# Window attention scores on 32-row tiles of TensorE over four PSUM banks, with a three-bank ring for the other products

## Chip, core and metric

The kernel runs on one core of a Trainium2 chip. The metric is the device time of one execution in microseconds. The engines are TensorE (PE in the rows; its weight loads are PEld), VectorE (DVE), ScalarE (ACT), GpSimd (POOL) and SyncE (SP). Each works through its own list of instructions in order, and they wait for each other through semaphores. TensorE writes its results into PSUM, eight banks of 128 partitions by 512 float32.

## What is computed

Four blocks run one after the other on x of 16 samples, 96 channels and 16 by 16 pixels, each as x = x + block(group_norm(x)): layer 0 is window attention with 12 heads of width 8, layer 1 shifted-window attention with 12 heads of width 32, then two blocks of convolution (layer 2) and spiking attention (layer 3), whose arithmetic the change leaves alone. A sample has four windows of 64 tokens.

```python
# layer 0, hd = 8
attn = jnp.einsum('bhnd,bhmd->bhnm', q * scale, k)
attn = jax.nn.softmax(attn + bias[None], axis=-1)
out = jnp.einsum('bhnm,bhmd->bhnd', attn, v)
out = out @ proj_w.T + proj_b
# layer 1, HD = 32, on x rolled by (-4, -4); masks in two of the windows' halves
dots = jnp.einsum('bhwid,bhwjd->bhwij', q, k) * SCALE
dots = dots + pos_emb[REL[..., 0], REL[..., 1]]
attn = jax.nn.softmax(dots, axis=-1)
out = jnp.einsum('bhwij,bhwjd->bhwid', attn, v)
out = out @ w_out + b_out
```

## The kernel before

Everything stays in SBUF after the loads at the start; eight stores end the run. All attention arithmetic is float32. The two attention layers form one chain of 32 steps, one per sample, that every engine walks through with its own function (`pe_sample`, `act_sample`, `dve_sample`, `pool_sample`; `attention_layers` calls them, and a loop of two samples each covers the regular middle of a layer). A step handles sample s and, to keep all engines busy, parts of its neighbours: prev = s-1, prev2 = s-2, nxt = s+1, nxt2 = s+2.

The four windows of a sample are two pairs, and each pair gives two groups of six heads: four groups w = 0 to 3, in halves j = 0 (w = 0, 1) and j = 1 (w = 2, 3). A group passes through these operations:

- scores (`pe_scores`, L900): 12 matmuls for each half, each on 64 rows by 64 columns of the array with 128 moving columns. The 64 rows hold more than one head, so k is copied from PSUM once per head with a mask that zeroes the others (`evac_k`, L1050), and in layer 0 q is copied three times with three masks (`evac_q`, L1038).
- bias add (`dve_bias`, L1099), row maximum (`dve_max`, L1103), subtraction of the maximum on GpSimd (`pool_shift`, L1141),
- transposition, three 128 by 128 blocks (`pe_transpose`, L909), exponential (`act_exp`, L1005),
- values (`pe_values`, L929: 12 matmuls of 128 by 64), division by the row sums (`dve_heads`: reciprocal L1126, multiply L1128), turning the result (`pe_turn`, L958), the output product (`pe_out`, L975 and L973), its bias (`act_out`), and the residual on GpSimd.

The products q, k and v of a coming sample (`pe_qkv`, L866 for q and k, L876 for v) are spread between these. PSUM: banks 0 and 1 hold scores, 2 and 3 the transposed probabilities (`ps_probsT`, used in turn), 4 the values (`ps_heads`), 5 and 6 the q, k and v products in turn (`ps_qkv`, `bank_of`), 7 everything else (`ps_mix`: turned heads, output product, statistics, weight preparation). One semaphore per `ps_qkv` bank (`evac_a`, `evac_b`) counts the copies out of it.

A float32 matmul stands as two MATMUL and two LDWEIGHTS records in the trace, a transposition as one of each. So a scores step has 24 records of either kind.

TensorE's order in a step: scores j=1; values j=1 of prev; v of nxt; (layer 1: turn j=0 of prev;) transpose 0; (layer 1: third qk product of nxt;) transpose 1; output product of prev2; scores j=0 of nxt; values j=0; (layer 1: second v product;) transpose 2; first product of nxt2; transpose 3; turn of prev; second product of nxt2. VectorE's order is bias 2 and 3, maximum 2, then in layer 0 the division of prev, maximum 3 and the two v copies of nxt (L1062), in layer 1 the v copies, maximum 3 and the division; then the same kind of work for the j=0 scores of nxt.

Some steps carry a job as well: the group-norm statistics of a half layer (0,1), (1,0), (1,1), (2,0), or a piece of weight preparation ("pos", "pw", "w3", "bn", "pwT"). Each has a part on VectorE before the bias adds of nxt (`dve_job_in`), a TensorE part in `ps_mix`, and a part on VectorE at the step's end.

## Time and profile before

| | us |
|---|---|
| median of 3 runs | 401.65 (399.36 to 402.13) |
| the profiled execution | 399.56 |
| its span | 397.8 |
| layer 0 steps, from the first j=1 scores of sample 0 | 24.1 to 140.4 |
| layer 1 steps, to the j=1 scores of the last sample | 140.4 to 306.9 |
| the rest of the span (layers 2 and 3, stores) | 306.9 to 397.8 |

TensorE is busy for 92% of the span, VectorE for 77%, ScalarE for 61%, GpSimd for 46%. A busy share adds up records, and TensorE's matmuls overlap, so its share alone doesn't say that it bounds the kernel. The timeline, which lists groups of equal instructions by start time with the idle time before them, shows whether one follows the other without a gap. Times in it are from the start of the span.

### The profile page before, as it was taken

What the parts mean: (1) busy time and instruction counts of PE and PEld (TensorE: products, weight loads), DVE (VectorE), ACT (ScalarE), POOL (GpSimd) and SP (SyncE); (2) the same over time, 40 slices, a digit from 0 to 9 for tenths busy, and PEclk for the clock granted to TensorE, in tenths of its full rate; (3) what the DMA queues carried; (4) which work ended last, traced back from release to release, by engine and by line L of the source; (5) the groups of instructions that cost most, each with busy time, mean ns of one, the idle gap of its engine ahead of it and who ended that gap; (6) DMA issues with size and microseconds to landing.
All of it is one profiled execution on the core that took longest, in us unless ns stands there. A gap on an engine that the chain in (4) does not pass through costs nothing.

```text
span 397.8 us, 13249 instructions
## 1 busy us (share of the span) xinstructions
PE 365.8 (92%) x4889; PEld 266.8 (67%) x4889; DVE 306.5 (77%) x721; ACT 243.7 (61%) x571; POOL 184.0 (46%) x325
## 2 busy tenths in 40 slices
PE   4579999999999997999999999999999999998893
PEld 1458878888878775877787777787777643334441
DVE  4887877878788679788977777787887949878774
ACT  5346666666756566456555666655556635559992
POOL 6765775756677444254443443443544334341000
PEclk9999999999999999899999999999999999999998
DMA  7700000000000000000000000000000000000112
GB/s 159 139 5 4 4 2 2 0 0 0 2 2 2 2 3 1 2 4 1 4 2 0 0 0 0 0 0 0 4 0 4 0 2 0 0 0 3 50 50 59
DMA packets 8505, 5.09 MB, mean 13 GB/s; under 512 B 5034, under 2 KB 8234, under 8 KB 8466
## 3 DMA queue, kind: packets, MB, share of 16 engines
q1 hardware_dynamic: 8306, 4.56, 5.2%
q8 instruction: 26, 0.43, 0.4%
q14 instruction: 13, 0.11, 0.1%
q10 hardware_dynamic: 160, 0.00, 0.0%
HBM read 2.98 MB, written 1.57 MB: 11 GB/s over the span
## 4 chain that ended last, share of the span: by engine, by line
PE 74%; DVE 11%; issue 4%; ACT 4%; POOL 0%; POOLq 0%; ACTq 0%; DVEq 0%
PE bank L929 12%; PE bank L900 12%; PE bank L866 11%; PE bank L909 10%; PE bank L1423 7%; PE bank L876 7%; PE bank L973 5%; PE bank L958 4%; DVE row_max L1103 2%; PE bank L1428 2%; DVE v L1062 2%; PE bank L1523 1%; PE bank L975 1%; ACT kvT L1556 1%; ACT count L1532 1%
## 5 line engine op out<-in xcount | busy, mean ns | idle before, releaser
L1141 POOL TENSOR_TENSOR probs<-probs,row_max 128x384 f32<-128x384 f32 x128 | 105.4, 829 | 115.0 <-DVE row_max L1103 114.2
L1005 ACT ACTIVATE probsT<-bank 128x384 f32<-128x384 f32 x128 | 61.1, 492 | 74.4 <-PE bank L909 74.4
L1099 DVE TENSOR_TENSOR probs<-bank,bias 128x384 f32<-128x384 f32 x128 | 65.4, 552 | 51.3 <-PE bank L900 49.9
L1103 DVE TENSOR_REDUCE row_max<-probs 128x6 f32<-128x384 f32 x128 | 68.4, 545 | 1.0
L909 PE MATMUL bank<-cst,probs 128*128 128x128 f32 x384 | 63.0, 281 | 0.0
L929 PE MATMUL bank<-v,probsT 128*64 128x18 f32 (+1 forms) x1536 | 58.1, 220 | 3.2 <-DVE headsN L1128 2.9
L929 PEld LDWEIGHTS bank<-v,probsT 128*64 128x64 f32 x1536 | 50.5, 138 | 14.7 <-issue 13.6
L900 PE MATMUL bank<-k,q 64*64 64x128 f32 x1536 | 56.7, 277 | 1.9 <-ACT k L1050 1.9
L900 PEld LDWEIGHTS bank<-k,q 64*64 64x64 f32 x1536 | 41.3, 132 | 22.0 <-issue 21.0
L1050 ACT ACTIVATE k<-bank,cst 128x256 f32<-128x256 f32 x128 | 54.0, 483 | 1.7 <-PE bank L866 1.7
L909 PEld LDWEIGHTS bank<-cst,probs 128*128 128x128 f32 x384 | 44.7, 142 | 11.2 <-issue 4.7
L1062 DVE COPY v<-bank 64x384 f32<-64x384 f32 (+1 forms) x96 | 46.8, 487 | 4.1 <-PE bank L876 1.8
L866 PE MATMUL bank<-xn,w 128*128 128x256 f32 x192 | 49.7, 381 | 0.0
L866 PEld LDWEIGHTS bank<-xn,w 128*128 128x128 f32 x192 | 32.8, 191 | 2.5
L1151 POOL TENSOR_TENSOR x<-y_attn,x_turned 96x96 f32<-96x96 f32 (+3 forms) x64 | 18.4, 317 | 25.8 <-ACT y_attn L1021 25.8
L1423 PE MATMUL bank<-pad,tapT 96*96 96x512 f32 x64 | 28.9, 594 | 0.0
L1010 ACT COPY heads<-bank 128x384 f32<-128x384 f32 x32 | 15.5, 484 | 21.4 <-PE bank L958 21.3
L876 PE MATMUL bank<-w,xn 128*64 128x192 f32 x256 | 27.2, 333 | 0.0
L1032 ACT ACTIVATE q<-bank 128x256 f32<-128x256 f32 x48 | 18.8, 391 | 12.4 <-PE bank L866 12.4
L866 PE MATMUL bank<-xn,w0T 128*128 128x256 f32 x64 | 20.4, 405 | 6.5 <-ACT xn L998 4.2
L958 PE MATMUL bank<-cst,headsN 128*128 128x128 f32 (+1 forms) x128 | 23.0, 282 | 3.6 <-DVE gn_veps L755 2.7
L1128 DVE TENSOR_TENSOR headsN<-bank,inv_sum 128x384 f32<-128x384 f32 (+1 forms) x48 | 23.6, 491 | 1.7
(147 smaller groups left out, 514.8 us busy)
## 6 DMA issues: line engine op xcount, KB each, us to landing
x<-in_x SPq DMA_DIRECT2D x4, 384.0 KB, 5.6
out_dram<-x SPq DMA_DIRECT2D x8, 192.0 KB, 2.1
w<-in_L_conv_w_qkv SPq DMA_DIRECT2D x1, 432.0 KB, 5.3
cst<-in_consts SPq DMA_DIRECT2D x1, 304.0 KB, 5.3
p<-in_L_conv_w_out SPq DMA_DIRECT2D x1, 144.0 KB, 5.1
pos<-in_L_conv_pos_emb SPq DMA_DIRECT2D x8, 2.0 KB
cst<-in_consts SPq DMA_DIRECT2D x1, 117.0 KB, 2.2
w_raw<-in_L_conv_qkv_w SPq DMA_DIRECT2D x1, 108.0 KB, 5.0
```

Of the source, the lines that this page charges most:

```text
L866: last = nc.tensor.matmul(o[:, half * T:(half + 1) * T], w[:, col:col + 128], xn[par][:, :], start=True, stop=True)
L876: last = nc.tensor.matmul(o[h * WT:(h + 1) * WT, at_ * n:(at_ + 1) * n], xn[par][:, w * WT:(w + 1) * WT], w_v[:, h], start=True, stop=True)
L900: one = nc.tensor.matmul(ps_scores[u][c * WT:(c + 1) * WT, p * 128:(p + 1) * 128], q, k, start=True, stop=True)
L909: last = nc.tensor.transpose(ps_probsT[w % 2][:, p * 128:(p + 1) * 128], probs[w][:, 2 * p:2 * p + 2, :], ident)
L929: last = nc.tensor.matmul(ps_heads[c * WT:(c + 1) * WT, at_:at_ + n], probsT[2 * j + u][:, p * 128 + c * WT:p * 128 + (c + 1) * WT], v, st ...
L1005: nc.scalar.activation(probsT[w][:, :], ps_probsT[w % 2][:, 0:NP * 128], ACT.Exp).then_inc(L.s.probsT_sb, 1)
L1050: return nc.scalar.activation(dst, src, ACT.Copy, scale=scale)
L1062: return nc.scalar.copy(dst, src) if eng == "act" else nc.vector.tensor_copy(dst, src)
L1099: nc.vector.tensor_tensor(out, scores, b, ALU.add).then_inc(L.s.biased, 1)
L1103: nc.vector.tensor_reduce(row_max[w][:, :], probs[w][:, :, :], AX.X, ALU.max).then_inc(L.s.maxed, 1)
L1141: nc.gpsimd.tensor_tensor(probs[w][:, :, :], probs[w][:, :, :], by_row(row_max[w]), ALU.subtract).then_inc(L.s.shifted, 1)
L1423: nc.tensor.matmul(o, tapT[:, t, :], tap_of(par, SUM_TAPS + t), start=(t == 0), stop=False)
```

## The change

Scores now use 32 rows by 64 columns of the array. In layer 1 those 32 rows are exactly one head, so q and k need no mask: one copy of 512 columns (`evac_qk`) takes the place of three copies of 256, and each half has 24 matmuls of 64 moving columns (48 records) instead of 12 of 128. In layer 0, 32 rows hold three heads: q is copied once, k three times with masks (before: q three times, k twice), and each half has 8 matmuls of 192 columns (16 records). Row groups of the array at work together write to different banks, so scores take four banks. The q scale moves into the weights: into the copy of layer 0's, and for layer 1 into one multiplication of 96 by 384 on GpSimd during step 0.

Four banks remain for the rest: one (not two) for the transposed probabilities, so each `pe_transpose` waits for the exponential before it, and three (`ps_a`, `ps_b`, `ps_c`) that all other products share in a fixed rotation, with one semaphore for each kind of use. `pe_bank_free` and the waits in `pe_turn`, `pe_out` and `pe_values` name the copy that must have emptied the bank. In layer 0 `ps_a` goes v of nxt, q of nxt2, turned heads of prev; `ps_b` output product, k; `ps_c` values. In layer 1 `ps_a` goes values j=1, third qk, second v, turn j=1; `ps_b` first v, output product, first qk; `ps_c` turn j=0, values j=0, second qk.

```diff
-        bank = [ctx.enter_context(nc.psum_tensor(f"bank{i}", [128, 512], F32)) for i in range(8)]
-        ps_scores = bank[0:2]
-        ps_probsT = bank[2:4]
-        ps_heads = bank[4]
-        ps_qkv = bank[5:7]
-        ps_mix = bank[7]
+        ps_scores = [ctx.enter_context(nc.psum_tensor(f"ps_scores{u}", [128, 2, 512], F32)) for u in range(NU)]
+        bank = [ps_scores[i // 2][:, i % 2, :] for i in range(4)]
+        bank += [ctx.enter_context(nc.psum_tensor(f"bank{i}", [128, 512], F32)) for i in range(4, 8)]
+        ps_probsT = bank[4]
+        ps_a, ps_b, ps_c = bank[5:8]
...
+        def pe_bank_free(pe, L, s, i):
...
+            if kind == "q":
+                if at:
+                    use_evacuated(pe, L0, moved(s, -1), "v")
+            elif kind == "k":
+                wait(pe, L0.s.y_ready, s + (-3) if at > 3 else 0)
...
             par = parity(s)
-            for p in range(NP):
+            blocks = range(NP) if L.wide else range(1)
+            n = WT if L.wide else TRIO * WT
+            for p in blocks:
                 for c in range(2):
                     w = 2 * j + c
-                    for u in range(NU):
...
+                    for r in range(NR):
+                        rows, cols = slice(r * ROWS, (r + 1) * ROWS), slice(w * WT, (w + 1) * WT)
+                        q = qk1[par][rows, p, 0, cols] if L.wide else q0[par][rows, cols]
+                        k = qk1[par][rows, p, 1, cols] if L.wide else k0[par][rows, w, :, :]
+                        one = nc.tensor.matmul(ps_scores[r // 2][c * WT:(c + 1) * WT, r % 2, p * n:(p + 1) * n], q, k,
                                                start=True, stop=True)
...
         def pe_transpose(pe, L, s, w):
             pe.wait_ge(L.s.shifted, win_count(s, w))
-            wait(pe, L.s.probsT_sb, win_count(s, w - 2))
+            wait(pe, L.s.probsT_sb, win_count(s, w - 1))
...
+            elif at < B - 2:
+                use_evacuated(pe, L1, moved(s, 2), *(("qk", 1) if j == 0 else ("v", 1)))
...
+        def evac_qk(L, s, i, j):
+
+            return nc.scalar.copy(qk1[parity(s)][:, j, :, :], bank_of(L, s, i)[:, :].rearrange("r (t q) -> r t q", t=2))
...
+            elif not L.wide:
+                if prev2:
+                    pe_out(pe, *prev2)
+                if not nxt2[0].wide:
+                    pe_qkv(pe, *nxt2, "q")
             pe_transpose(pe, L, s, 1)
...
             one(B, "pw")
-            one(B + 1, "w3")
+            one(B + 1, "bn")
             one(B + 2, (1, 1))
-            one(B + 3, "bn")
-            loop(L1, 4, B - 4)
+            one(B + 3, "w3")
+            one(B + 4, "split")
+            one(B + 5, "dw")
+            loop(L1, 6, B - 4)
```

The `elif` shown third from the end is in `pe_turn` (layer 1). ScalarE normalises nxt2 at the start of a layer 0 step, not after its second exponential, and copies q before k. A job's TensorE part now stands after the scores of nxt, its first VectorE part where it was, and its second right after the bias adds of nxt; the long chains of small VectorE operations ("bn", now 6 operations; the three-way "split" of layer 3's weights; the 9 of "dw"; 7 of "pw") stand at the end of their steps, ahead of the statistics: in steps 16 ("pw"), 17 ("bn"), 20 ("split") and 21 ("dw"). In layer 2 the accumulator of the taps moves to banks 2 and 3, so that the first tap of pair 0 can start inside the last attention step.

On TensorE, a step of layer 0 outside the loop (sample 2), from the values of prev on. L900 is scores, L929 values, L876 the v product, L909 transpositions, L975 the output product, L866 a q or k product, L958 turned heads. Before:

```order
L929 MATMUL bank<-v_1,probsT 64x18 x12
L876 MATMUL bank<-w0T,xn 64x48 x8
L909 MATMUL bank<-cst,probs 128x128 x6
L975 MATMUL bank<-heads_0,p0T 96x256
L900 MATMUL bank<-k_1,q_1 64x128 x12
L929 MATMUL bank<-v_0,probsT 64x18 x12
L909 MATMUL bank<-cst,probs 128x128 x3
L866 MATMUL bank<-xn,w0T 128x256
L909 MATMUL bank<-cst,probs 128x128 x3
L958 MATMUL bank<-cst,headsN 96x128 x2
L866 MATMUL bank<-xn,w0T 128x256
L900 MATMUL bank<-k_1,q_1 64x128 x12
```

After (L953 scores, L987 values, L925 v, L964 transpositions, L1040 output, L915 q or k, L1019 turned heads):

```order
L987 MATMUL bank<-v_1,probsT 64x18 x12
L925 MATMUL bank<-w0T,xn 64x48 x8
L964 MATMUL bank<-cst,probs 128x128 x3
L1040 MATMUL bank<-heads_0,p0T 96x256
L915 MATMUL bank<-xn,w0T 128x256
L964 MATMUL bank<-cst,probs 128x128 x3
L953 MATMUL ps_scores<-k_1,q_1 64x192 x8
L987 MATMUL bank<-v_0,probsT 64x18 x12
L964 MATMUL bank<-cst,probs 128x128 x3
L915 MATMUL bank<-xn,w0T 128x256
L1019 MATMUL bank<-cst,headsN 96x128 x2
L964 MATMUL bank<-cst,probs 128x128 x3
```

The next row after either list belongs to the next step. The q product of nxt2, which was the L866 after transposition 2, stands between transpositions 0 and 1, behind the output product; the k product and the turned heads stand ahead of transposition 3, which now has nothing between it and the next step's scores.

On VectorE, one step of layer 1 without its statistics (L1099 bias adds, L1103 maximum, L1062 v copies, L1126 and L1128 division). Before:

```order
L1099 TENSOR_TENSOR probs<-bank,bias 128x384 x2
L1103 TENSOR_REDUCE row_max<-probs 128x6
L1062 COPY v_0<-bank 64x12x32 x2
L1103 TENSOR_REDUCE row_max<-probs 128x6
L1126 RECIPROCAL inv_sum<-bank 128x12
L1128 TENSOR_TENSOR headsN<-bank,inv_sum 128x384
L1099 TENSOR_TENSOR probs<-bank,bias 128x384 x2
L1103 TENSOR_REDUCE row_max<-probs 128x6
L1062 COPY v_0<-bank 64x12x32 x2
L1103 TENSOR_REDUCE row_max<-probs 128x6
L1126 RECIPROCAL inv_sum<-bank 128x12
L1128 TENSOR_TENSOR headsN<-bank,inv_sum 128x384
```

After (L1154 bias adds, L1158 maximum, L1116 v copies, L1170 and L1172 division):

```order
L1154 TENSOR_TENSOR probs<-ps_scores,bias 128x2x3x64 x2
L1170 RECIPROCAL inv_sum<-bank 128x12
L1172 TENSOR_TENSOR headsN<-bank,inv_sum 128x384
L1116 COPY v_1<-bank 64x12x32 x2
L1158 TENSOR_REDUCE row_max<-probs 128x6 x2
L1154 TENSOR_TENSOR probs<-ps_scores,bias 128x2x3x64 x2
L1170 RECIPROCAL inv_sum<-bank 128x12
L1172 TENSOR_TENSOR headsN<-bank,inv_sum 128x384
L1116 COPY v_1<-bank 64x12x32 x2
L1158 TENSOR_REDUCE row_max<-probs 128x6 x2
```

The division and the two v copies now come ahead of both maxima. In layer 0 the order on VectorE is the same as before.

## Rows read from the trace of the kernel before

**Rows 1.** Page, busy time of each engine, us (share of the span) xinstructions
```profile
PE 365.8 (92%) x4889; PEld 266.8 (67%) x4889; DVE 306.5 (77%) x721; ACT 243.7 (61%) x571; POOL 184.0 (46%) x325
```

**Rows 2.** Windows of two stages; columns: window, length, busy time (xinstructions), PEclk, DMA, GB/s
```profile
core 0: us, PE busy (x) PEld busy (x) DVE busy (x) ACT busy (x) POOL busy (x), PEclk, DMA share, GB/s
24.10:140.40 116.30, 113.76 (x2106) 92.81 (x2105) 90.66 (x223) 75.75 (x192) 74.14 (x127) 1.00 0.01 2
140.40:306.90 166.50, 162.08 (x2216) 128.07 (x2215) 131.65 (x296) 98.09 (x255) 71.12 (x126) 0.99 0.01 1
```

**Rows 3.** Timeline, PE, one sample of layer 0; columns: start us, us, engine, line, operation
```profile
86.68 0.89 PE L900 MATMUL bank<-k,q 64*64 64x128 f32 x24
87.50 0.88 PE L929 MATMUL bank<-v,probsT 128*64 128x18 f32 x24
...
88.80 0.88 PE L909 MATMUL bank<-cst,probs 128*128 128x128 f32 x6
...
91.66 0.55 PE L909 MATMUL bank<-cst,probs 128*128 128x128 f32 x3
...
92.48 0.49 PE L909 MATMUL bank<-cst,probs 128*128 128x128 f32 x3
92.81 0.38 PE L958 MATMUL bank<-cst,headsN 128*96 128x128 f32 x2
93.02 0.60 PE L866 MATMUL bank<-xn,w0T 128*128 128x256 f32 x2
93.55 0.89 PE L900 MATMUL bank<-k,q 64*64 64x128 f32 x24
```

**Rows 4.** Timeline, DVE, the same stretch; brackets: idle before it and who ended it
```profile
87.62 1.02 DVE L1099 TENSOR_TENSOR probs<-bank,bias 128x384 f32<-128x384 f32 x2 [1.16 <-PE bank L900]
...
90.08 0.73 DVE L1062 COPY v<-bank 64x192 f32<-64x192 f32 x2
```

**Rows 5.** Source view, one scores step; matmul ns min/median/max, first to last start
```profile
L900 PE MATMUL bank<-k,q x24: 269/269/320, 252.4 to 253.1; 64*64 64x128 f32 x24
```

**Rows 6.** Source view, the values step of layer 0 at 87.50
```profile
L929 PE MATMUL bank<-v,probsT x24: 211/211/232, 87.5 to 88.2; 128*64 128x18 f32 x24
```

**Rows 7.** Timeline, PE, only the first 0.16 us of that scores step
```profile
252.44 0.34 PE L900 MATMUL bank<-k,q 64*64 64x128 f32 x4
```

**Rows 8.** Timeline, PE, one sample of layer 1
```profile
254.76 0.55 PE L958 MATMUL bank<-cst,headsN 128*128 128x128 f32 x3
...
256.34 0.49 PE L909 MATMUL bank<-cst,probs 128*128 128x128 f32 x3
...
258.05 0.89 PE L900 MATMUL bank<-k,q 64*64 64x128 f32 x24
...
261.95 0.49 PE L958 MATMUL bank<-cst,headsN 128*128 128x128 f32 x3
...
263.24 0.89 PE L900 MATMUL bank<-k,q 64*64 64x128 f32 x24
```

**Rows 9.** Timeline, DVE, the second half of that sample
```profile
259.08 1.02 DVE L1099 TENSOR_TENSOR probs<-bank,bias 128x384 f32<-128x384 f32 x2 [1.62 <-PE bank L900]
260.02 0.54 DVE L1103 TENSOR_REDUCE row_max<-probs 128x6 f32<-128x384 f32 x1
260.49 1.14 DVE L1062 COPY v<-bank 64x384 f32<-64x384 f32 x2
...
262.25 0.23 DVE L1126 RECIPROCAL inv_sum<-bank 128x12 f32<-128x12 f32 x1
262.52 0.56 DVE L1128 TENSOR_TENSOR headsN<-bank,inv_sum 128x384 f32<-128x384 f32 x1
```

**Rows 10.** Timeline, ACT, the first exponential of that sample
```profile
255.76 0.49 ACT L1005 ACTIVATE probsT<-bank 128x384 f32<-128x384 f32 x1
```

**Rows 11.** Timeline, PE, the stall in a layer 0 sample with a normalisation job
```profile
51.92 0.42 PE L958 MATMUL bank<-cst,headsN 128*96 128x128 f32 x2 [0.95 <-DVE gn_veps L755]
```

**Rows 12.** Timeline, PE, the stall in the sample with job w3
```profile
158.78 1.32 PE L929 MATMUL bank<-v,probsT 128*64 128x66 f32 x24 [1.38 <-DVE headsN L1128]
```

More of the change, by code:

```diff
@@ L111, in v_index @@
     def v_index(self, j):
-        return [i for i, use in enumerate(self.plan) if use[0] == "v"][j if self.wide else 0]
+        return self.index("v", j if self.wide else 0)
     def rank(self, i):
@@ L712, in build, with norm_bank @@
         HB = B // 2
+        def norm_bank(layer, half):
+            return ps_c if (layer, half) >= (2, 1) else ps_b
         def gn_count(layer, half):
@@ L1064, in evacuate @@
[L1064 to L1082 removed]
+            return nc.vector.tensor_copy(dst, src)
```

557 lines of the change are left out of this document (297 added, 260 removed).

## Prediction

> **What bounds the kernel now.** I read the page first: TensorE (PE) is busy for 92% of the span, VectorE (DVE) for 77% [rows 1]. Then the windows, which split the span: layer 0's 16 steps take 116.3 us, layer 1's 15 up to the last j=1 scores 166.5 us [rows 2]; 90.9 us of the span lie behind them. The change acts on the first two. Their clock is 1.00 and 0.99 of full speed, the upper of its two levels (2.4 GHz), so nothing is to be won there.
>
> The timeline of one sample shows what the shares don't. In layer 0 TensorE's groups follow each other with no idle time marked; a step lasts 93.55 - 86.68 = 6.87 us [rows 3]. In layer 1 it is 263.24 - 252.44 = 10.80 us [rows 7, 8]. VectorE waits in both for scores, 1.16 us at one place in layer 0 [rows 4] and 1.62 us at one in layer 1 [rows 9]. So TensorE's own list sets both layers, and any time taken out of it counts in full, until a wait takes its place. The question is what the new waits cost.
>
> **Scores.** A step has two scores groups, each 0.82 us from its start to that of the next group [rows 3]. Its 24 records have their last start 0.89 - 0.27 = 0.62 us after the first [rows 5, 8]. With four tiles at work that is six rounds of 0.11 us, and 128 moving columns set the round. Four matmuls of 0.32 us are over after 0.34 us [rows 5, 7], so a start follows another by 0.02/3 = 0.007 us. Eight tiles then need 0.05 us to start. The other floor on a round is the reload of a tile's weights: layer 0's values, with only 18 moving columns in two tiles, have 12 rounds in 0.88 - 0.21 = 0.67 us, 0.06 us each [rows 3, 6].
> - Layer 1 after: 48 records are six rounds of eight. The stream of 64 columns takes 0.055 us, the weights 0.06. Last start at about 0.40 us, and the next group 0.15 us later (0.20 now, less 0.05 of stream): 0.55 instead of 0.82, 0.27 less.
> - Layer 0 after: 16 records, two rounds of 192 columns, 0.16 us each: last start at 0.26, next group 0.25 later: 0.51, 0.30 less.
>
> No row shows a 32-row tile. The bounds: no round gets shorter because weights or banks serialise (0.82 stays), or all floors vanish (another 0.1 off each). I take the values above, since the four-tile row and the weight row lie next to it.
>
> A rule of the Trainium skill, "TensorE: Matmul & The Clock Gate", section "Wait — 56ns, not 53.3ns?", speaks against the change: matmul starts are never closer than about 25 ns, however few columns. With 48 records that would be an estimated 1.2 us for a layer 1 group, longer than now. The trace disagrees for different tiles: its four starts lie within 0.02 us [rows 5, 7]. It is a rival below, priced from rows.
>
> Both scores together take 0.60 us off layer 0's step (6.27) and 0.54 off layer 1's (10.26).
>
> **Copies.** ScalarE does less: in layer 1 three copies for each sample instead of nine, in layer 0 four instead of five. ScalarE was waiting often, so this gives nothing by itself. VectorE's work is the same in kind and size.
>
> **Layer 0: the q product waits for the v copies.** This is the decisive edit. q of nxt2 goes into the bank that v of nxt has just filled, in the same step, and waits until VectorE has copied v out. VectorE does that last: bias adds, maximum, division, maximum, v. Now, a step's scores start at 86.68, the first bias add at 87.62, the v copies end at 90.08 + 0.73 = 90.81, 4.13 us after the scores [rows 3, 4]. With scores 0.30 shorter it is 3.83, plus 0.05 for the semaphore (the gap from the end of scores, 87.57, to the bias add, 87.62) and 0.05 for the load of the first weights: q can run at 3.93. In TensorE's list q stands at 88.80 - 86.68 - 0.30 = 1.82 (scores, values, v), plus transposition and output product. Both together are as long as transposition 2 and the k product, 92.48 - 91.66 = 0.82 [rows 3], of which 0.38 is the transposition. That is 2.64. TensorE has nothing else that it may run: transposition 1, the next scores and all behind them stand after q in its list. Wait: 1.3 us.
>
> Three short ones come from the single bank of transposed probabilities and the new places. A transposition, its exponential and two semaphores take 0.49 + 0.04 + 0.49 + 0.05 = 1.07 us [rows 3, 10]. Transpositions 1 and 3 now have only scores between them and the values that need that exponential: 0.33 for a transposition, 0.51 for the scores and 0.09 that it costs to go from full to small tiles (the product ahead of scores takes 93.55 - 93.02 = 0.53, the other 0.44): 0.93 [rows 3]. That is 0.14 short, twice; one of the two lies ahead of q and is absorbed there. Transposition 3 waits for exponential 2: here 0.06 more for a transposition that comes first (0.55 against 0.49) and 0.05 for weights, 1.18, against 0.82 for transposition and k product and 0.21 for the turned heads, 1.03 [rows 3]: 0.15. Together: 1.29 + 0.14 + 0.15 = 1.58, so the step is 6.27 + 1.6 = 7.87 us, 1.0 us longer. VectorE's 90.66/16 = 5.7 us of work [rows 2] fit.
>
> Fourteen steps (samples 0 to 13) issue a q: +14.0. Steps 0 and 1 lack work that now fills TensorE and then hides in the wait: +0.8, an estimate. The two normalisation steps stall 0.95 us now [rows 11]; their VectorE part moves into time in which VectorE waits anyway: -1.0 each. Steps 14 and 15 have no q: -0.3. Layer 0: +12.5.
>
> **Layer 1.** Here v copies and division move ahead of the maxima, and that is needed: turn j=1 takes the bank of the second v. From the j=0 scores: bias adds start 0.76 later (1.03 now [rows 8, 9], less 0.27), then 0.94 for two (260.02 - 259.08), 0.27 and 0.48 for the division (the next operation starts 0.08 before the multiply's 0.56 are over, as behind the bias adds), 1.14 for v, 0.1 for semaphore and weights: 3.69 [rows 9]. TensorE's list has 261.95 - 258.05 - 0.27 = 3.63 [rows 8]: 0.06 late. Transposition 1 needs exponential 0, which ends at 256.25, 1.49 after turn j=0, plus 0.1 = 1.59 against 256.34 - 254.76 = 1.58 [rows 8, 10]: 0.01. The step is 10.26 + 0.07 = 10.33 us, 0.46 less. VectorE's load is 131.65/15.4 = 8.5 us [rows 2], with gaps about 8.9: 1.4 free. What is late next is turn j=1; GpSimd has half its time free. Fifteen steps: -6.9.
>
> Jobs: the 1.38 us stall of w3 [rows 12] goes, and the other job steps lose about as much together: -3. The chains at their new ends (1.5 to 2.4 us each on an engine with 1.4 free) cost 2. Layer 1: -8.0. One ScalarE copy less at the start and the earlier first tap: -0.3. The GpSimd multiplication lands in time in which GpSimd waits.
>
> **Sum.** 12.5 - 8.0 - 0.3 = +4.2 on the profiled execution's 399.6 (span 397.8 and 1.8 around it): 403.8. The median lies 2.1 above that execution, so 405.9; I say 406.
>
> **Rivals.**
> - The v copies don't hold q up. They would have to end 2.5 us after the scores start instead of 3.83, or q have another bank. Then layer 0's step is 6.27 + 0.43 = 6.70, 0.17 less: -2.4 - 2.0 and -8.3 make 389. It is the case that ends faster. Against it: the list is strict and 3.83 is made of measured durations. 0.10.
> - The short waits don't appear or overlap: 14 x 0.43 less, 400. For it: they are of the size of my reading errors. 0.18.
> - VectorE becomes layer 1's bound: with 8.9 of 10.33 us, two late releases of 0.25 us, or dearer bias adds over two banks, eat the gain of 0.46: 406 + 6.9 = 413. 0.15.
> - The tiles don't run eight wide. If rounds stay at 0.11 us: 14 x 0.6 + 15 x 0.5 = 16 more, 422. If starts can't be closer than 0.67/23 = 0.029 us, as in the values' 24 records [rows 3, 6], a layer 1 group takes 47 x 0.029 + 0.15 = 1.5 us, 1.0 more, 30 times, and layer 0's 0.18 more: 406 + 30 + 5 = 441. This is the mechanism that the rule above would have. 0.12 together.
>
> **Chances.** The forecast has 0.45. The range 398 to 414 takes in the forecast, the short waits and VectorE's case, and leaves out 0.22 less the milder half of the eight-wide case. One per cent is about what a measurement can tell: 397.6 and 405.7. Faster: the first rival and a bit of the second, 0.14. Slower: half of the forecast, VectorE's case and the tiles, 0.50. Same: 0.36.
>
> **What would show it.** Right: in layer 0, TensorE idle more than 1 us ahead of L915, released by VectorE's v copy (L1116), in each step, and a step near 7.9 us; a scores step of 16 records with last start near 0.26 us, one of 48 near 0.40; layer 1's step near 10.3 us with waits below 0.1 at the turned heads (L1019). Wrong: no idle at L915, a layer 1 scores group longer than 0.8 us, or layer 1 at 10.8 with TensorE waiting for L1116 or L1172.

## The result, and the profile after

The changed kernel takes 425.37 us (median of 4 runs, 420.61 to 426.95) against 400.5: 5.9% slower (ratio 1.0593, 95% interval 1.0537 to 1.065; ratios leave out runs more than 1.5% above the kernel's fastest, here the profiled one). The forecast of 406 had the sign, and not the size; its range ended at 414. The profiled execution took 426.95, its span is 425.2. Mean granted clocks of the four executions: 0.956, 0.960, 0.972 and 0.984, the fastest with the highest.

The page first, busy time and the granted clock in 40 slices:

```profile
PE 374.7 (88%) x5401; PEld 260.3 (61%) x5401; DVE 305.2 (72%) x721; ACT 218.0 (51%) x459; POOL 183.3 (43%) x326
...
PEclk9955599999999999999999999999999999999996
```

TensorE's busy share has fallen from 92% to 88% [rows 1], and the clock, which was at full speed throughout layer 0 [rows 2], stands at half in the third to fifth slice. Windows of the three stages, then of the stretch with the low clock; columns as in [rows 2]:

```profile
core 0: us, PE busy (x) PEld busy (x) DVE busy (x) ACT busy (x) POOL busy (x), PEclk, DMA share, GB/s
24.59:166.45 141.86, 124.15 (x1883) 89.50 (x1882) 90.53 (x222) 72.55 (x173) 73.74 (x128) 0.90 0.01 1
166.45:333.00 166.55, 159.37 (x2932) 124.62 (x2931) 131.55 (x299) 77.18 (x165) 69.39 (x125) 1.00 0.01 2
333.00:425.20 92.20, 79.17 (x473) 39.48 (x472) 66.55 (x156) 58.59 (x101) 22.30 (x30) 0.96 0.06 18
```

```profile
22.40:53.10 30.70, 28.41 (x274) 20.63 (x275) 14.91 (x37) 10.80 (x26) 12.65 (x16) 0.50 0.01 2
```

Layer 0 takes 141.9 us instead of 116.3, layer 1 166.6 instead of 166.5, the rest 92.2 instead of 90.9, and 0.5 more lie ahead. So 25.6 of the 27.4 us lost are in layer 0, and layer 1 didn't pay for them. The clock of TensorE is at its lower level, 1.2 GHz, for 30.7 us, from 22.40 on.

One regular step of layer 0, TensorE. It begins at 89.98 and ends at 98.34:

```profile
89.98 0.58 PE L953 MATMUL ps_scores<-k,q 32*64 32x192 f32 x16
90.63 0.88 PE L987 MATMUL bank<-v,probsT 128*64 128x18 f32 x24
...
92.32 0.59 PE L1040 MATMUL bank<-heads,p0T 128*96 128x256 f32 x2
93.89 0.70 PE L915 MATMUL bank<-xn,w0T 128*128 128x256 f32 x2 [0.97 <-DVE v L1116]
94.42 0.49 PE L964 MATMUL bank<-cst,probs 128*128 128x128 f32 x3
94.84 0.58 PE L953 MATMUL ps_scores<-k,q 32*64 32x192 f32 x16
95.57 0.88 PE L987 MATMUL bank<-v,probsT 128*64 128x18 f32 x24
96.38 0.55 PE L964 MATMUL bank<-cst,probs 128*128 128x128 f32 x3
...
97.68 0.52 PE L964 MATMUL bank<-cst,probs 128*128 128x128 f32 x3
98.34 0.58 PE L953 MATMUL ps_scores<-k,q 32*64 32x192 f32 x16
```

The idle time of 0.97 ahead of q, released by the v copy (L1116), is the forecast wait. VectorE and ScalarE in the same step:

```profile
93.10 0.73 DVE L1116 COPY v<-bank 64x192 f32<-64x192 f32 x2
```

```profile
94.95 0.49 ACT L1074 ACTIVATE probsT<-bank 128x384 f32<-128x384 f32 x1 [1.45 <-PE bank L964]
```

The v copies end at 93.83, q starts at 93.89, 3.91 us after the scores (3.93 forecast). The exponential of transposition 1 starts 0.53 after it and ends at 95.44; the values that need it start at 95.57, 1.15 after the transposition.

Layer 1, TensorE, and the start of one scores group seen through a window that ends 0.28 us into it:

```profile
263.76 0.78 PE L953 MATMUL ps_scores<-qk 32*64 32x64 f32 x48
264.47 0.92 PE L987 MATMUL bank<-v,probsT 128*64 128x66 f32 x24
```

```profile
263.76 0.49 PE L953 MATMUL ps_scores<-qk 32*64 32x64 f32 x32
```

and through one that ends 0.04 us into it:

```profile
263.76 0.30 PE L953 MATMUL ps_scores<-qk 32*64 32x64 f32 x7
```

A group of 48 records is followed by the values after 0.71 us (0.82 before [rows 3], 0.55 forecast); its first 32 records start within 0.28, its first 7 within 0.04.

### The profile page after: what moved, and what is told of

It is laid out like the page before. It is cut to its first block, busy times and chain, and to the rows that moved or that the text cites. A ratio compares the mean times of both kernels' runs of the same rounds, so it can differ in the third digit from the quotient of the medians.

```text
span 425.2 us, 14132 instructions
## 1 busy us (share of the span) xinstructions
PE 374.7 (88%) x5401; PEld 260.3 (61%) x5401; DVE 305.2 (72%) x721; ACT 218.0 (51%) x459; POOL 183.3 (43%) x326
## 3 DMA queue, kind: packets, MB, share of 16 engines
HBM read 2.98 MB, written 1.57 MB: 11 GB/s over the span
## 4 chain that ended last, share of the span: by engine, by line
PE 65%; DVE 15%; issue 7%; ACT 6%; POOL 1%; DVEq 0%; POOLq 0%; ACTq 0%
PE bank L915 13%; PE bank L987 11%; PE bank L964 10%; PE ps_scores L953 7%; PE ps_scores L1503 6%; PE bank L1038 5%; PE bank L925 4%; DVE row_max L1158 4%; PE bank L1019 3%; DVE v L1116 3%; ACT probsT L1074 3%; DVE probs L1154 2%; PE ps_scores L1508 2%; ACT kvT L1636 1%; ACT count L1612 1%
## 5 line engine op out<-in xcount | busy, mean ns | idle before, releaser
L1154 DVE TENSOR_TENSOR probs<-ps_scores,bias 128x384 f32<-128x384 f32 x128 | 65.4, 553 | 79.5 <-PE ps_scores L953 76.8
L964 PE MATMUL bank<-cst,probs 128*128 128x128 f32 x384 | 69.6, 292 | 2.8 <-ACT probsT L1074 2.1
L1158 DVE TENSOR_REDUCE row_max<-probs 128x6 f32<-128x384 f32 x128 | 65.8, 545 | 1.1
L987 PE MATMUL bank<-v,probsT 128*64 128x18 f32 (+1 forms) x1536 | 60.1, 223 | 3.2 <-ACT probsT L1074 1.0
L987 PEld LDWEIGHTS bank<-v,probsT 128*64 128x64 f32 x1536 | 52.6, 142 | 15.8 <-ACT probsT L1074 8.4
L964 PEld LDWEIGHTS bank<-cst,probs 128*128 128x128 f32 x384 | 44.3, 146 | 20.8 <-issue 16.7
L915 PE MATMUL bank<-xn,w 128*128 128x256 f32 x192 | 49.9, 382 | 5.7 <-DVE headsN L1172 5.5
L1116 DVE COPY v<-bank 64x384 f32<-64x384 f32 (+1 forms) x96 | 46.5, 484 | 2.0 <-PE bank L925 0.5
L915 PE MATMUL bank<-xn,w0T 128*128 128x256 f32 x64 | 24.3, 471 | 19.4 <-DVE v L1116 14.9
L1106 ACT COPY qk<-bank 128x512 f32<-128x512 f32 x48 | 28.1, 585 | 21.8 <-PE bank L915 21.8
L915 PEld LDWEIGHTS bank<-xn,w 128*128 128x128 f32 x192 | 32.7, 190 | 9.5 <-issue 5.7
L1503 PE MATMUL ps_scores<-pad,tapT 96*96 96x512 f32 x64 | 28.9, 594 | 0.0
L915 PEld LDWEIGHTS bank<-xn,w0T 128*128 128x128 f32 x64 | 11.6, 222 | 26.2 <-issue 13.2
L953 PEld LDWEIGHTS ps_scores<-qk 32*64 32x64 f32 x1536 | 20.6, 131 | 11.2 <-issue 11.2
L925 PE MATMUL bank<-w,xn 128*64 128x192 f32 x256 | 26.3, 327 | 0.0
L953 PE MATMUL ps_scores<-qk 32*64 32x64 f32 x1536 | 25.0, 232 | 0.2
L1172 DVE TENSOR_TENSOR headsN<-bank,inv_sum 128x384 f32<-128x384 f32 (+1 forms) x48 | 23.6, 491 | 1.6
L1038 PE MATMUL bank<-heads,p 128*96 128x256 f32 x96 | 23.3, 379 | 0.0
```

The costliest lines, as they stand in the source:

```text
L915: last = nc.tensor.matmul(o[:, at_ * T:(at_ + 1) * T], w[:, col:col + 128], xn[par][:, :], start=True, stop=True)
L925: last = nc.tensor.matmul(o[h * WT:(h + 1) * WT, at_ * n:(at_ + 1) * n], xn[par][:, w * WT:(w + 1) * WT], w_v[:, h], start=True, stop=True)
L953: one = nc.tensor.matmul(ps_scores[r // 2][c * WT:(c + 1) * WT, r % 2, p * n:(p + 1) * n], q, k, start=True, stop=True)
L964: last = nc.tensor.transpose(ps_probsT[:, p * 128:(p + 1) * 128], probs[w][:, 2 * p:2 * p + 2, :], ident)
L987: last = nc.tensor.matmul(heads_bank(L, j)[c * WT:(c + 1) * WT, at_:at_ + n], probsT[2 * j + u][:, p * 128 + c * WT:p * 128 + (c + 1) * WT ...
L1038: last = nc.tensor.matmul(o, p1[:, p, :], heads1[parity(s)][:, p, :], start=(p == 0), stop=(p == NP - 1))
```

## The experiments

Each ran beside the kernel before on the same chip, so ratios are to that.

**1. q behind the scores of nxt.**

```diff
             if nxt:
                 pe_scores(pe, *nxt, 0)
+            if nxt and not nxt[0].wide and not nxt2[0].wide:
+                pe_qkv(pe, *nxt2, "q")
...
-                if not nxt2[0].wide:
-                    pe_qkv(pe, *nxt2, "q")
             pe_transpose(pe, L, s, 1)
```

> The changed kernel with one edit: in layer 0 the q product of nxt2 stands behind the scores of nxt, not behind the output product. Measured before the edit: the output product's last start to q's first is 1.35 and 1.57 us in alternate samples, against 0.22 without a wait. Theory A (q waits for the v copies): at its new place, about 0.4 (transposition) + 0.5 (scores) later, the v copies are nearly done, and q also fills the wait of values j=0 for exponential 1; the step falls from 8.3 to 7.2 us or less, 14 steps, 424 to about 408. Rival B (TensorE would wait there anyway, for the exponentials or for VectorE): the wait moves to the values and the step stays above 8.0, total within 4 us of the changed kernel. On the clock: if it is the idle time within each step of layer 0 that keeps the clock low, its low stretch gets shorter here too and another 5 to 8 us go.

Measured: 420.21 us, ratio 1.0461 (1.0384 to 1.0539). TensorE, from scores j=0 to scores j=0 of the next sample:

```profile
101.80 0.58 PE L953 MATMUL ps_scores<-k,q 32*64 32x192 f32 x16
...
109.12 0.58 PE L953 MATMUL ps_scores<-k,q 32*64 32x192 f32 x16
```

That is 7.32 us; the regular steps alternate between 7.19 and 7.55, mean 7.4 instead of 8.3. The mechanism holds, and the wait is worth 0.9 to 1.0 us for each step. The total missed the 408 that I expected. In the profiles steps 3 to 13 gained 8.0 us, but steps 0 to 2 ran at half clock in this kernel too (12.67, 11.75 and 9.07 us) and gained nothing there, step 0 began 1.6 us later, and step 21 took 14.51 us instead of 12.82, with the clock at half for part of it. The first low stretch got no shorter: 30.7 us again.

**2. The order of layer 0 rewritten.**

```diff
             pe_scores(pe, L, s, 1)
+            if nxt and not nxt[0].wide:
+                pe_qkv(pe, *nxt, "v", 0)
+                pe_transpose(pe, L, s, 0)
+                if prev:
+                    pe_values(pe, *prev, 1)
+                if prev2:
+                    pe_out(pe, *prev2)
+                pe_transpose(pe, L, s, 1)
+                pe_scores(pe, *nxt, 0)
+                if not nxt2[0].wide:
+                    pe_qkv(pe, *nxt2, "q")
...
+                pe_transpose(pe, L, s, 2)
+                pe_values(pe, L, s, 0)
...
+                pe_qkv(pe, *nxt2, *(("qk", 0) if nxt2[0].wide else ("k", 0)))
+                if prev:
+                    pe_turn(pe, *prev, 1)
+                pe_transpose(pe, L, s, 3)
```

> The changed kernel with layer 0's order alone rewritten. TensorE: scores j=1, v of nxt, transposition 0, values j=1 of prev, output product, transposition 1, scores j=0, q, transposition 2, values j=0, k, turned heads, transposition 3. VectorE: bias adds, maximum 2, v copies, maximum 3, division. Measured spacings behind it: 1.30 us from a transposition's start to that of the next when only its exponential is between, 1.15 us to the values. In this order the shortest ways are 1.6 and 1.5 us, and v is copied out 2.9 us after the scores start, with q at about 3.7. Theory A (the waits, q's and the single bank's, are all that layer 0 lost): a step falls from 8.3 to 6.3 to 6.5 us, under the 6.87 of the kernel before, so layer 0 takes about 106 us at full clock. Theory A for the clock (thin steps are what keeps it low once it has fallen): with a step as dense as before the low stretch ends after at most 10 us, total about 395 us. Rival B (the clock depends on the stretch ahead of step 0 alone): the same low stretch of 30 us, total about 402. Rival C (VectorE or ScalarE bound the step once the waits go): a step stays above 7 us, total above 405.

Measured: 412.02 us, ratio 1.0322 (1.0248 to 1.0396). Two starts of scores j=1, one sample apart:

```profile
89.03 0.58 PE L953 MATMUL ps_scores<-k,q 32*64 32x192 f32 x16
...
92.36 0.58 PE L953 MATMUL ps_scores<-k,q 32*64 32x192 f32 x16
92.88 0.70 PE L915 MATMUL bank<-xn,w0T 128*128 128x256 f32 x2
93.41 0.49 PE L964 MATMUL bank<-cst,probs 128*128 128x128 f32 x3
...
95.82 0.58 PE L953 MATMUL ps_scores<-k,q 32*64 32x192 f32 x16
```

The step is 6.78 us in every regular sample, with no wait of TensorE: 1.5 us less than in the changed kernel, and 0.09 less than before. So the two waits, q's and the single bank's, are all that a regular step of layer 0 had lost against the kernel before. A scores group takes 92.88 - 92.36 = 0.52 us, as forecast (0.51). But the step is not the 6.3 to 6.5 that I expected, and the rows say where the rest went: the q product, between scores on small tiles and a transposition, takes 93.41 - 92.88 = 0.53, where the one between two transpositions took 0.44 [rows 3]. The four transpositions, each now with another tile size beside it, take 1.73 us instead of 1.42. I read this as about 0.1 for each change between tile sizes, of which the rewritten order has more; no run varies that alone.

The clock wasn't what I expected: the profile has a low stretch of 17.1 us, and the four executions have means of 0.959 to 0.979, though the steps are as dense as before. Steps 0 and 1, the first of them at half clock, take 7.6 us more than before, which is most of the 9.5 us that layer 0 is longer, and the total isn't the 395 to 402 that I expected.

**3. Idle time ahead of step 0.** TensorE is idle 2.64 us ahead of the q product of sample 1 (2.24 in the kernel before), and 0.78 us behind the first scores of step 0, where v of sample 1 waits for ScalarE's copy of q:

```profile
23.47 1.19 PE L915 MATMUL bank<-xn,w0T 128*128 128x256 f32 x2 [2.64 <-DVE v L1116]
24.59 0.94 PE L953 MATMUL ps_scores<-k,q 32*64 32x192 f32 x16
26.31 1.09 PE L925 MATMUL bank<-w0T,xn 128*64 128x48 f32 x16 [0.78 <-ACT q L1096]
```

The clock falls at 22.40 here, inside the first of these stretches, so the second, which the change added, didn't start this fall; it could still have kept the clock low. In the profile of the split scores (experiment 5) it falls at 25.3, inside the second. Seven kernels test whether idle time at this place brings the low clock on.

```diff
             pe_qkv(pe, L0, 1, "k")
-            pe_qkv(pe, L0, 1, "q")
...
             pe_scores(pe, L, s, 1)
+            if not prev:
+                pe_qkv(pe, L0, 1, "q")
```

> The changed kernel with one edit ahead of the first step: the q product of sample 1 stands behind the first scores of step 0 instead of ahead of them, so TensorE's idle stretch of 2.64 us, in which the granted clock fell to 0.50 (and stayed there for 30.7 us of the 425 us), is cut to about 1.5 us. Theory A (that stretch of idle time starts the fall): the clock stays at 1.00 through layer 0, steps 0 to 2 take 8.3 us and not 11.96, 11.16 and 9.04, total about 8.5 us less than with the fall, 416 to 418. Rival B (the thinner work of the steps themselves makes the clock fall, sooner or later): it still falls within the first steps, total 424.

Measured: 422.0 us, ratio 1.0535 (1.0458 to 1.0612), mean clocks 0.960, 0.984, 0.984 and 0.985. In the profile the low stretch lasts 6.8 us, and steps 1 and 2 take 8.05 us each instead of 11.16 and 9.04: that is the price of half clock for these steps. One execution in four, at 427.39 us and a mean clock of 0.960, suggests that the long low stretch still comes. The same edit on the rewritten order:

> The kernel of the run before with one more edit, the q product of sample 1 behind the first scores of step 0. It shortens TensorE's idle time ahead of step 0 by about 1 us. If the start of the low stretch hangs on that idle time, 1 to 8 us less than the kernel of the run before, by whether that one has a low stretch at all; if not, the same within 1 us.

Measured: 410.72 us, ratio 1.0291 (1.0229 to 1.0354), clocks 0.963, 0.971, 0.975, 0.996: no clear difference, and the profile has 17.1 us at half clock again. The edit shortens the first idle stretch and lengthens the second (v waits 1.65 us), so it decides nothing. Nor do the times follow the clock here: the execution at 0.996 took 411.91 us, those at 0.971 and 0.975 took 409.54 and 408.89.

Filler, which takes both idle stretches away (11 and 5 matmuls; L1416 in the trace):

```diff
+        def pe_fill(pe, n):
+            pe.wait_ge(dve_prep, done["bias_half"])
+            for _ in range(n):
+                nc.tensor.matmul(ps_c[:, 0:T], w0T[:, 0:128], xn[1][:, :], start=True, stop=True)
...
+            pe_fill(pe, 11)
             pe_qkv(pe, L0, 1, "q")
...
             pe_scores(pe, L, s, 1)
+            if not prev:
+                pe_fill(pe, 5)
```

> The changed kernel with filler matmuls, whose results nobody reads, in TensorE's two idle stretches around the first scores of step 0: 11 full matmuls ahead of the q product of sample 1 (idle 2.64 us there) and 5 ahead of v of sample 1 (idle 0.78 us). So far 12 of 16 executions of kernels built on the changed one had a mean clock of 0.975 or less, with a low stretch of 17 to 31 us that starts there; none of 18 of the kernel before had one. Theory A (the idle stretches there start it): the clock stays at 1.00 through the first steps, mean 0.985 or more in nearly all executions; step 0 about 8.6, steps 1 and 2 8.1 us; total 416 to 419. Rival B (the way that layer 0's steps use TensorE starts it, or holds it): low stretches as before, total 421 to 427.

(The count in that text is wrong: it was 16 of 23 executions with a mean clock of 0.975 or less.) Measured: 424.15 us, ratio 1.061 (1.0569 to 1.065). The mean clock did what theory A says, 0.984 to 0.996 in all six executions; the total didn't. The trace shows why:

```profile
21.04 4.91 PE L1416 MATMUL bank<-xn,w0T 128*128 128x256 f32 x22
...
26.83 2.43 PE L1416 MATMUL bank<-xn,w0T 128*128 128x256 f32 x10
29.18 0.67 PE L925 MATMUL bank<-w0T,xn 128*64 128x48 f32 x16
```

The filler is longer than the idle time: v of sample 1 starts at 29.18, not at 26.31. And the low clock isn't gone, only later and shorter. It falls during a q wait of 1.50 us that ends at 39.71, in step 1:

```profile
39.40:46.20 6.80, 6.49 (x55) 4.97 (x55) 2.10 (x5) 1.47 (x4) 2.68 (x4) 0.51 0.01 2
```

With the filler on the rewritten order:

> The rewritten order of layer 0 (step 6.78 us, total 409 to 414, low stretch of 17 us in its profile) with the same filler. Theory A: no low stretch, 4 to 6 us less, 403 to 406. Rival B: 409 to 414 as without it.

408.62 us, ratio 1.0232 (1.0196 to 1.0268), clocks 0.983 to 0.997. Then with 5 and 2 fillers:

> The changed kernel with less filler: 5 matmuls ahead of the q product of sample 1 and 2 ahead of v, not 11 and 5. In the trace of the run with 11 and 5, eleven fillers lasted 4.8 us (0.44 each, twice what I had taken) and filled more than the idle time: v of sample 1 started at 29.18 us, not 26.31, which is 2.9 us of the kernel's own making. With 5 and 2 (2.2 and 0.9 us) they end before what TensorE waits for. Theory (the low clock costs the changed kernel about 7 us, and the long filler gave half of it back): mean clock 0.984 or more in nearly all executions, 418 to 421. If the total stays at 424, the low stretch is not what costs those microseconds.

> The rewritten order of layer 0 with 5 and 2 fillers instead of 11 and 5 (408.6 us with those): 2 to 3 us less, 405 to 407, mean clock 0.984 or more. If it is 408 to 409 again, the filler's length was hidden anyway.

On the changed kernel: 422.45 us, ratio 1.0505 (1.0452 to 1.0558). Its executions line up by their mean clock: 418.10 us at 0.996, 419.37 at 0.992, 421.99 to 423.26 at 0.984 to 0.987, 425.88 at 0.975. On the rewritten order: 406.4 us, ratio 1.0159 (1.0116 to 1.0202), 404.35 to 409.07. By the one execution at 0.996, the changed kernel without a long low stretch takes about 418, some 7 us less than its median. The profile of 5 and 2 still has 6.8 us at half clock in step 1 (10.74 us), which begins around a q wait of 1.50.

The reverse, the idle time put into the kernel before:

```diff
-            pe_qkv(pe, L0, 1, 0, 2)
+            pe_qkv(pe, L0, 1, 0, 1)
+            pe.wait_ge(L0.s.maxed, win_count(0, 1))
+            pe_qkv(pe, L0, 1, 1, 2)
...
             pe_scores(pe, L, s, 1)
+            if not prev:
+                pe.wait_ge(L0.s.maxed, win_count(0, 2))
```

> The kernel before with two waits at its start, which give TensorE the idle time that the changed kernel has there: the q or k product of sample 1 waits 0.6 us longer (idle about 2.8 us in all) and v of sample 1, behind the first scores, waits about 0.8 us. Theory A (idle time around the first scores of step 0 starts the low stretch): some executions fall to a mean clock of 0.98 or less and lose up to 8 us; the rest 402 to 403. Rival B (the order and the small tiles of layer 0 do it): the mean clock stays between 0.985 and 0.996, 402 to 403.

Measured: 406.68 us, ratio 1.0144 (1.0102 to 1.0186). Its first scores, its first idle stretch, its second, and the window with the low clock:

```profile
18.99 1.56 PE L900 MATMUL bank<-k,q 64*64 64x128 f32 x24
20.48 0.67 PE L876 MATMUL bank<-w0T,xn 128*64 128x48 f32 x16
...
23.93 1.22 PE L866 MATMUL bank<-xn,w0T 128*128 128x256 f32 x2 [2.15 <-DVE row_max L1103]
...
28.28 1.09 PE L876 MATMUL bank<-w0T,xn 128*64 128x48 f32 x16 [1.65 <-DVE row_max L1103]
```

```profile
23.60:40.70 17.10, 15.13 (x148) 11.62 (x149) 5.90 (x15) 5.21 (x12) 5.41 (x8) 0.51 0.01 1
```

Idle 2.15 and 1.65 us, and the clock is at half for 17.1 us in a kernel whose steps and tiles are those of before. Four of the six executions have mean clocks of 0.975 to 0.979 and take 406.19 to 407.38; two have 0.985 and 0.987 and take 403.14 and 403.81. None of the 36 executions of the kernel before that ran beside these experiments was below 0.985. Rival B falls: a low stretch at the start needs neither the small tiles nor the new order, and the two added waits bring it on. How they do is not shown. In this profile the clock falls at 23.6, inside the first stretch, which at 2.15 us is no longer than the 2.24 of the kernel before, whose clock stayed up; the two waits weren't tried one by one. TensorE had also run its first scores at half pace (20.48 - 18.99 = 1.49 us, 0.82 in the kernel before) where PEclk says 1.00, so ahead of about 24 us that column can't be taken at its word.

**4. One of the waits in the kernel before.**

```diff
                 pe_out(pe, *prev2)
+            if nxt and not nxt[0].wide and not nxt2[0].wide:
+                evacuated(pe, *nxt, L0.v_index(0))
             if nxt:
                 pe_scores(pe, *nxt, 0)
```

> The kernel before with one wait added in steps 0 to 13: ahead of the scores of nxt, TensorE waits until the v copies of nxt are done. Nothing else differs; the scores stay on 64 by 64 tiles. In its trace the scores of nxt start 3.35 us after those of j=1, and the v copies end 4.13 after them, plus 0.1: a wait of 0.9 us for each, 14 times 0.9 = 12 us, 413. Theory A (thin steps, not the 32-row tiles, keep the clock low): some executions also show a low stretch of more than 10 us within the first 60 us, and up to 8 us more. Rival B (the small tiles do it): mean clock stays at 0.985 or above in all executions, 413 us.

Measured: 413.55 us, ratio 1.035 (1.0314 to 1.0387), clocks 0.973, 0.989, 0.990, 0.991, 0.996. The wait:

```profile
92.20 0.34 PE L900 MATMUL bank<-k,q 64*64 64x128 f32 x4 [1.04 <-DVE v L1062]
```

A step is 7.98 us instead of 6.87. Idle time of 1.04 us in each step costs what it lasts, 14 us in all, and the profile has no low clock in layer 0. So such waits needn't start a low stretch: four executions of five are at 0.989 or more. The fifth, at 0.973 and 417.29 us, is unexplained, and it isn't a rule: with filler the clock fell in a q wait of 1.50 us, and in the profiles of the rewritten order with filler it is at half for 3.4 us, some 2 us behind waits of 1.34 and 1.35 us for the statistics (L791).

**5. What limits a layer 1 scores group.** Scores twice, then half the moving columns:

```diff
-            for p in blocks:
+            for again, p in [(i, p) for i in range(2 if L.wide else 1) for p in blocks]:
...
```

> The changed kernel with layer 1's scores issued twice (same result): 96 records a group instead of 48. In the changed kernel the first 32 starts of a group come in bursts of eight every 0.055 us (0.266 us for 32), the rest one every 0.0167 us, 0.564 us in all. Theory A (after some 32 records TensorE gets its instructions only at one pair of records per 0.0167 us): the group's starts spread over 0.27 + 64 x 0.0167 = 1.34 us, the step 1.6 us longer. Rival B (the tiles set the pace and the second half is slower for a reason inside a group): 2 x 0.564 = 1.13 us, step 1.1 us longer. Rival C (a tile's round is 0.055 us, the tail a one-off): 0.564 + 6 x 0.055 = 0.89, step 0.7 us longer.

```diff
-                        k = qk1[par][rows, p, 1, cols] if L.wide else k0[par][rows, w, :, :]
+                        k = qk1[par][rows, p, 1, w * WT:w * WT + WT // 2] if L.wide else k0[par][rows, w, :, :]
+                        m = WT // 2 if L.wide else n
...
```

> The changed kernel with 32 instead of 64 moving columns in each of layer 1's scores matmuls; half of its scores are left out, so the output is another one. 48 records as before. Theory A (supply of instructions sets the second half of the group): the group's starts still spread over at least 0.5 us. Rival B (the moving columns set the rounds): the rounds of 0.055 us become 0.03, the group 0.3 us or less.

One group and the values behind it, of the one and of the other:

```profile
305.16 1.25 PE L953 MATMUL ps_scores<-qk 32*64 32x64 f32 x96
306.35 0.92 PE L987 MATMUL bank<-v,probsT 128*64 128x66 f32 x24
```

```profile
268.62 0.73 PE L954 MATMUL ps_scores<-qk 32*64 32x32 f32 x48
269.28 0.92 PE L988 MATMUL bank<-v,probsT 128*64 128x66 f32 x24
```

96 records take 1.19 us to the values (0.71 for 48), and the step grows from 10.74 to 11.69: 0.475 for each 48 more; the starts spread over 1.03. Half the columns save 0.05 of 0.71. So the columns don't set the pace. Theory A's 1.34 was too long, its rate of one pair in 0.0167 us isn't held throughout; 0.475/48 = 0.0099 is the mean of what follows. The 1.03 measured lies between rival B's 1.13 and rival C's 0.89, so none of the three describes it. (These kernels ran once each: 452.31 and 425.03 us, the second with half of layer 1's scores left out.) The third run cuts a group in two:

```diff
+            if L.wide and nxt:
+                pe_scores(pe, *nxt, 0, (0, 1))
             if prev2 and (L.wide or nxt[0].wide):
                 pe_out(pe, *prev2)
             if nxt:
-                pe_scores(pe, *nxt, 0)
+                pe_scores(pe, *nxt, 0, (1, 9) if L.wide else (0, 9))
```

(and likewise for j=1, ahead of the last qk product of a step)

> The changed kernel with each layer 1 scores group (48 records) cut in two: 16 records stand ahead of the product before it (two to six full matmuls), 32 behind it. Twice the records (96 in a group) took 1.03 us and half the columns 0.50 against 0.56, so it is neither the columns nor a growing price. Theory A (TensorE has some 32 record pairs at hand and then gets them slower than the tiles could take them; long matmuls let it catch up): both parts run at 0.0085 us a start, spread 0.13 and 0.27, together 0.40 instead of 0.56; with 0.1 for one more change between tile sizes the step is 0.1 to 0.2 us shorter. Rival B (the second half of a group is slow because tiles or banks wait for each other): the part of 32 records is as slow as records 17 to 48 were, 0.40 or more, and the step gets longer by 0.2.

```profile
271.27 0.38 PE L954 MATMUL ps_scores<-qk 32*64 32x64 f32 x16 [0.58 <-ACT qk L1107]
...
277.11 0.37 PE L954 MATMUL ps_scores<-qk 32*64 32x64 f32 x16
277.41 1.13 PE L915 MATMUL bank<-xn,w 128*128 128x256 f32 x4
278.47 0.49 PE L954 MATMUL ps_scores<-qk 32*64 32x64 f32 x32
278.88 0.92 PE L988 MATMUL bank<-v,probsT 128*64 128x66 f32 x24
```

The part of 32 records now takes 0.41 to the values, 0.30 less than a whole group, and the one of 16 takes 0.30 to the product: the later records of a group are as fast as its first when other work lies between. The starts of the 32 spread over 0.49 - 0.22 = 0.27 us (0.22 is one record), where rival B expected 0.40 or more: it falls. A supply of instructions that slows down fits; so would something behind the tiles that fills up and empties during the other work, which no run excludes. The step got longer, not shorter (442.31 us in all, one execution): the early part of scores j=0 waits 0.58 us for ScalarE's third qk copy, which I had overlooked, and two more changes of tile size come with it.

**6. VectorE's chains in layer 1.** In the changed kernel TensorE has four idle stretches of about 1 us or more in layer 1, all ahead of the third qk product (L915) and all released by the division of values j=1 (L1172):

```profile
181.01 1.10 PE L915 MATMUL bank<-xn,w 128*128 128x256 f32 x4 [1.43 <-DVE headsN L1172]
...
192.13 1.10 PE L915 MATMUL bank<-xn,w 128*128 128x256 f32 x4 [0.98 <-DVE headsN L1172]
...
227.67 1.10 PE L915 MATMUL bank<-xn,w 128*128 128x256 f32 x4 [2.01 <-DVE headsN L1172]
...
239.59 1.13 PE L915 MATMUL bank<-xn,w 128*128 128x256 f32 x4 [1.06 <-DVE headsN L1172]
```

```profile
222.05 0.75 DVE L659 CAST w_parts<-w_rest 97x384 bf16<-97x384 f32 x1
...
225.31 0.42 DVE L739 BATCH_NORM_STATS2 stats<-x 96x6 f32<-96x256 f32 x1
```

```profile
269.68 1.02 DVE L1154 TENSOR_TENSOR probs<-ps_scores,bias 128x384 f32<-128x384 f32 x2 [0.87 <-PE ps_scores L953]
```

They sum to 5.5 us, one behind each of pw, bn, split and dw. The chain split holds VectorE from 222.05 to 225.31, 3.3 us; and in a regular step VectorE waits at that place only 0.87 us (the last row), not the 1.4 that I had counted.

> The kernel of the run before with two chains of small VectorE operations in layer 1, split (3.3 us in a row in the trace of the changed kernel) and dw (2.5 us), each cut in two and spread over steps 20 to 23 instead of 20 and 21. VectorE waits 1.5 to 1.7 us for scores at that place of a regular step. If the chains' length beyond that wait is what they cost (TensorE idle 2.01 and 1.06 us after them in the changed kernel), 2.5 to 3 us less than the kernel of the run before; if it is the number of small operations, the same time.

Measured: 408.13 us, ratio 1.0219 (1.0173 to 1.0264), against 408.62 without the spreading, where 2.5 to 3 us were expected; one execution of the six, at a clock of 0.969, took 414.48. TensorE's longest idle time behind the four pieces:

```profile
219.39 1.10 PE L917 MATMUL bank<-xn,w 128*128 128x256 f32 x4 [1.01 <-DVE headsN L1174]
```

With 0.62, 0.32 and 0.45 behind the others that is 2.40 us instead of 3.07. Spreading moves the loss rather than ending it: each piece alone is longer than the 0.87 us of cover. I had taken VectorE's wait of 1.5 to 1.7 us at the other half of the step for the one at this place.

## Why the prediction was wrong

The forecast's own sum was 403.8 for the profiled execution; it took 426.95. Of the 23.2 us between, 13.1 are in layer 0 (25.6 longer, 12.5 forecast), 8.1 in layer 1, the rest at the two ends.

- **Layer 0's q wait: right.** Forecast 1.29 us; q starts 3.91 us after the scores (3.93). From the output product to q it is 93.89 - 92.32 = 1.57 us in the step shown and 1.79 in the next, where 0.44 would do: a wait of 1.13 and 1.35. Experiment 1 shows it by its removal.
- **The short waits: right kind, too small.** Behind q a step has 4.45 us where the forecast had 3.94. The terms "1.07" and "1.18" for a way through transposition and exponential are 1.15 and 1.30: I took 0.04 to 0.05 us for each semaphore where the rows show 95.57 - 95.44 = 0.13 ahead of the values; the product that follows a wait or small tiles costs 0.10 more; and every second sample's scores come about 0.2 late behind transposition 3, for a reason that stays open (it is gone in experiments 1 and 2). Step 8.3 against 7.87: about 5 us over layer 0.
- **The clock: missing from the sum.** The prediction said that nothing is to be won there, and didn't ask what could be lost. TensorE runs at half clock for 30.7 us, in which steps 0 to 2 take 11.96, 11.16 and 9.04 us instead of about 8.4, 8.05 and 8.05: 7 to 8 us. That the waits around the first scores of step 0 bring it on is shown in both directions: a mean clock of 0.975 or less in 16 of 23 executions of the changed kernel and its variants without filler and in 2 of 30 with it; 0.979 or less in 4 of 6 of the kernel before with gaps and in none of 36 without. The prologue had 2.24 us of idle time already; the change made it 2.64 and added 0.78. Which of the two counts, and why it comes in some executions only, stays open. The prediction looked at regular steps and never at this place, although the wait of v on the copy of q in the first samples was part of the diff.
- **Layer 1: scores 0.71 us, not 0.55.** The term "six rounds of eight, last start at about 0.40" failed. The rounds are as fast as I said for the first 32 starts (within 0.28 us), and the 16 behind them are slower. Experiment 5 excludes the columns and a pace that the tiles keep whatever lies between; that TensorE gets its instructions too slowly there is my guess, which no row shows by itself. The step gains 0.06 us instead of 0.46: 0.22 from the scores, of which waits take 0.16 back (0.07 forecast). About 6 us over 15 steps. Where the 0.16 of waits lie I read from the trace only.
- **Layer 1's chains: cost 5.5 us of idle time, not 2.** The mis-sized term is "an engine with 1.4 free"; the cost is read from the trace, and experiment 6 moved only 0.67 us of it. The stall of w3 did go: step 17 takes 11.56 us instead of 14.07. In that step of the kernel before 3.4 us ran at half clock; without them its layer 1 takes 165.3 us, as in the profiles of experiments 3 and 4 made from it, so the changed layer 1 is 1.3 us slower, not equal.
- **The rest** is 1.3 us longer (92.2 against 90.9) where 0.3 less was forecast. Most of it belongs to this one execution: in the profiles of experiments 1 to 3 made from the changed kernel the same part takes 91.1 to 91.3 us. Here the clock is at half for the last 6.9 us of the span, there for the last 2.7 to 3.9 (3.2 in the kernel before).

Of the rivals, the tiles "not eight wide" came nearest in mechanism and is wrong in detail: starts 0.007 us apart do occur, among the first 32 records. By the Trainium skill, "TensorE: Matmul & The Clock Gate", section "Wait — 56ns, not 53.3ns?", starts never come closer than about 25 ns. For matmuls on different tiles, of which that section doesn't speak, the runs show otherwise: 48 in a row average 0.012 us (0.56 us over 47). VectorE as layer 1's bound didn't happen in regular steps, only behind the chains.

No version made here beats the kernel before. The best, the rewritten order with 5 and 2 fillers, is 1.6% slower. The tiles of 32 rows save 0.3 us for each scores group in layer 0, and four banks for scores cost more than that in waits and changes of tile size, unless the order is rewritten; then it is a draw in the regular step, with the start and the job steps still dearer.

## To carry to other kernels

When a resource that was doubled becomes single, write down the way through it (here transposition, exponential, values: 1.15 us, and 1.30 back to the next transposition) and check every pair of uses in the order against it, before counting what the freed resource brings. Look at the first steps apart from the regular ones: waits of TensorE just ahead of its dense work can cost more in granted clock than in time, and cheap filler matmuls of the right length show how much. And count records, not only columns: a long run of small matmuls can go on more slowly than it starts.

## What the runs showed of the hardware

- Small float32 matmuls on eight tiles of 32 by 64 start as near as 0.007 us apart (7 within 0.04 us), and the first 32 of a run within 0.28; 48 more behind the first 48 cost 0.475 us, 0.0099 each. A group of 48 with 32 columns took 0.66 us, with 64 columns 0.71. Behind four to six records of full matmuls the first 32 are fast again.
- The same product took 0.44 us to the next group between transpositions and 0.53 behind small tiles.
- The same kernel doesn't always get the same clock: with gaps at the start, four of six executions had mean clocks of 0.975 to 0.979 (17.1 us at half clock in the profiled one), two had 0.985 and 0.987. A step of the changed kernel takes 11.16 us at 1.2 GHz and 8.05 at 2.4 GHz.
- What ends a low stretch stays open. TensorE was busy for 28.4 of its 30.7 us (busy shares at half clock), and the first low stretch of a profile lasted 3.4, 6.8, 17.1, 23.9, 27.3 or 30.7 us.
